# Four blocks of experts 0 to 3, with tokens of the first eleven tiles, ranked, gathered and begun ahead of the routing of the rest

## What is computed

```python
x = x + tanh(g_xattn) * xattn(layernorm(x), ctx, ctx, mask)      # 16 heads, 77 context rows
# _ffn on layernorm(x), B*S = 2048 tokens, E = 8 experts, D = 256, F = 1024
logits = xt @ Wr + br
gates  = max(softmax(logits)); idx = argmax(softmax(logits))     # top-1 routing
xn     = layernorm(xt) * ln_g + ln_b
h      = relu(xn @ W1[idx] + b1[idx])
y      = (h @ W2[idx] + b2[idx]) * gates
x = x + tanh(g_ffn) * y
```

## Time and profile before

| | |
|---|---|
| median of 3 runs | 311.1 us (309.79 to 313.14) |
| profiled execution | 310.44 us, of which the span of the core is 308.6 us |
| mean granted TensorE clock | 0.965 |
| PE busy | 280.3 us, 91% |
| DVE busy | 193.1 us, 63% |
| ACT busy | 163.2 us, 53% |
| POOL busy | 137.6 us, 45% |

### The profile page before, as it was taken

One profiled execution on the slowest core, in us unless ns is written; L12 is line 12 of the kernel. 1 busy time (PEld: TensorE's weight loads), 2 busy tenths in 40 slices (PEclk: granted clock), 3 DMA queues, 4 the chain that ended last, 5 costly groups with the idle time before them and its releaser, 6 DMA issues.

```text
span 308.6 us, 7697 instructions
## 1 busy us (share of the span) xinstructions
PE 280.3 (91%) x2489; PEld 249.3 (81%) x2489; DVE 193.1 (63%) x640; ACT 163.2 (53%) x439; POOL 137.6 (45%) x265
## 2 busy tenths in 40 slices
PE   7899998999999999999476999999999999999980
PEld 3668887888888888888234999888899989999970
DVE  3578589989999999886883653433435443445540
ACT  2243566767767777674316694434255725544440
POOL 2425247777777755434424653222232543322221
PEclk9999999999999999997777999999999999999996
DMA  6999994100103555551124303111121112112120
GB/s 139 295 296 372 377 379 135 54 37 35 37 36 129 174 202 173 179 170 43 37 75 135 101 11 88 54 30 48 52 56 55 50 54 57 54 59 80 55 58 14
DMA packets 19851, 34.59 MB, mean 112 GB/s; under 512 B 2518, under 2 KB 14612, under 8 KB 19801
## 3 DMA queue, kind: packets, MB, share of 16 engines
q1 hardware_dynamic: 15513, 21.28, 21.3%
q0 software_dynamic: 4144, 12.62, 13.0%
q10 hardware_dynamic: 144, 0.07, 0.1%
HBM read 27.60 MB, written 6.75 MB: 111 GB/s over the span
## 4 chain that ended last, share of the span: by engine, by line
PE 60%; DVE 24%; issue 6%; DMA 3%; ACT 2%; POOL 2%; SPq 1%; DVEq 1%; POOLq 0%; ACTq 0%
PE pS L1638 22%; PE pB L1709 15%; DVE mx L849 5%; PE pB L1445 4%; PE pA L1338 4%; PE pB L1426 4%; DVE Pb L857 3%; PE pT L1338 3%; DMA cst<-in_consts_dram 2%; DVE xs L879 2%; DVE st L884 1%; DMA zin<-rows_dram,idxg 1%; DVE xh L827 1%; PE pS L1382 1%; PE pA L1361 1%
## 5 line engine op out<-in xcount | busy, mean ns | idle before, releaser
L1638 PE MATMUL pS<-znf,W1c 128*128 128x128 f32 x576 | 72.2, 280 | 0.4 <-DVE W1c L1221 0.4
L1638 PEld LDWEIGHTS pS<-znf,W1c 128*128 128x128 f32 x576 | 68.7, 196 | 3.2 <-issue 3.2
L1709 PE MATMUL pB<-W2p,hT 128*128 128x256 f32 x408 | 53.7, 286 | 0.0
L1242 DVE TENSOR_SCALAR hA<-pS,b1s 128x128 f32<-128x128 f32 x72 | 20.3, 344 | 51.8 <-PE pS L1638 38.6
L1709 PEld LDWEIGHTS pB<-W2p,hT 128*128 128x128 f32 x408 | 50.0, 190 | 1.4 <-issue 1.2
L408 POOL DMA_INDIRECT out_dram<-yo,idxs x17 | 17.7, 1039 | 72.6 <-DVE yo L1270 63.9
L724 ACT ACTIVATE hA<-pS,b1s 128x128 f32<-128x128 f32 x72 | 20.6, 368 | 46.4 <-PE pS L1638 46.4
L1426 PE MATMUL pB<-VB,PT 128*128 128x51 f32 (+1 forms) x320 | 37.8, 273 | 0.4 <-DVE xs L879 0.3
L1426 PEld LDWEIGHTS pB<-VB,PT 128*128 128x128 f32 (+1 forms) x320 | 36.9, 192 | 1.4 <-issue 1.2
L567 ACT ACTIVATE Pb<-Pb 128x616 f32<-128x616 f32 x32 | 23.0, 718 | 17.3 <-DVE Pb L857 17.1
L391 POOL DMA_INDIRECT zin<-rows_dram,idxg x21 | 20.8, 992 | 16.5 <-issue 11.3
(11 more groups left out here) (233 smaller groups left out, 490.5 us busy)
## 6 DMA issues: line engine op xcount, KB each, us to landing
W1s<-in_L_ffn_W_dram SPq DMA_DIRECT2D x8, 1024.0 KB, 9.8
W2s<-in_L_ffn_W_dram SPq DMA_DIRECT2D x8, 1024.0 KB, 10.9
rows_dram<-pay POOLq DMA_DIRECT2D x16, 260.0 KB, 2.5
xs<-in_x_dram SPq DMA_DIRECT2D x3, 512.0 KB, 7.8
W2s<-in_sel_dram SPq DMA_DIRECT2D x1, 385.0 KB
zin<-rows_dram,idxg POOLq DMA_INDIRECT x21, 3.3
out_dram<-yo,idxs POOLq DMA_INDIRECT x17
W1s<-in_L_xattn_wk_dram SPq DMA_DIRECT2D x1, 256.0 KB, 3.1
```

Of the source, the lines that this page charges most:

```text
L1638: t = e.matmul(pS[:, 2 * (s % 2) + n, 128 * c:128 * c + 128], W1c[k][n][:, 128 * c:128 * c + 128], znf[s % 2][:, 128 * k:128 * k + 128], s ...
L1709: t = e.matmul(o, hT[s % 2][a][:, 128 * c:128 * c + 128], W2p[b_][c // 2][:, D * (c % 2):D * (c % 2) + D], start=False, stop=(c == 7 and a ...
```

## The change

Slots 0 to 3 become fixed: slot s is the first block of expert s (KA = 4), filled only with tokens of the first GA = 11 tiles, and only if these tiles hold at least 128 tokens of that expert. Otherwise its token numbers are all "none", and the slot is run all the same. The other slots are worked out as before over NL = 21 slots, with the counts less what the first blocks took; the total layout has NS = 25 slots, of which slots 4 and up start again at expert 0. The small path is hosted two slots behind the fixed ones (HOST = 6).

- The first group of ranks covers 11 tiles and moves into the loop (n = 13 on PE and DVE), with a product of counts for it; the key comparison for the four blocks (`first_values`) is in n = 14.
- `first_ids` on PE sits inside the `attend` of the last tile; then POOL gathers the four blocks between the steps of the last tiles' `rstd2` and `store_row`.
- The splits of W2 for slots 0 to 3 are done each time, pieces 1 to 3 on POOL and piece 0 on DVE; W1 is read without a copy.
- The work of slots 0 to 3 is written in between the steps of the routing of the rest, on all engines.
- SBUF buffers are reordered so that those of the first slots do not lie over attention's. Slots 0 to 4 share one pair of `hA` buffers.

```diff
-NS = 21
+KA = 4
+NL = 21
+NS = KA + NL
 FIRST = 14
-NK = NS + E
+NK = NL + E
+GA = NT - 5
-HOST = 2
+HOST = KA + 2
-WARM = (6, 3, 6, 9)
+WARM = (6, 3, 4)
...
-        groups = ((0, NT - 4), (NT - 4, NT - 1), (NT - 1, NT))
+        groups = ((0, GA), (GA, NT - 1), (NT - 1, NT))
...
 # POOL, after the loop
+            for x_ in range(KA):
+                e.wait_ge(d_W[x_], 32)
+            W2_low(0, 1)
+            e.wait_ge(g["dve_idxg"], 1)
+            for n in range(3):
+                i = GA - 1 - n
+                e.wait_ge(rsem[i % 3], 16 * (i // 3 + 1))
+            gather(0)
             rstd2(y)
+            gather(1)
+            gather(2)
+            rstd2(z)
             store_row(y - 1)
-            rstd2(z)
+            e.wait_ge(g["pe_PV"], NT)
+            gather(3)
             store_row(y)
             store_row(z)
+            W2_low(0, 2)
+            W2_low(0, 3)
+            for c in range(1, 4):
+                W2_low(1, c)
-            e.wait_ge(g["dve_idxg"], 1)
+            e.wait_ge(g["dve_idxg"], 2)
...
-            for s in range(4):
-                gather(s)
+            gather(KA)
+            gather(KA + 1)
+            e.wait_ge(g["dve_idxs"], 1)
+            scatter(0)
+            for c in range(1, 4):
+                W2_low(2, c)
+            scatter(1)
+            gather(KA + 2)
             e.wait_ge(g["dve_slot"], 1)
+            for c in range(1, 4):
+                W2_low(3, c)
+            scatter(2)
+            gather(KA + 3)
...
 # ACT, after the loop
+            copy_OT(y)
+            copy_PT(z, 0)
...
+            W2_high(0, 0)
+            W2_high(0, 1)
+            copy_PT(z, 1)
+            copy_PT(z, 2)
...
+            gate_exp(y)
+            W2_high(0, 2)
+            W2_high(0, 3)
+            x2_row(z)
+            e.wait_ge(g["dve_lnb"], 1)
+            layer_in(0)
+            z_row(z)
+            layer_in(1)
+            gate_exp(z)
+            e.wait_ge(g["dve_b1"], 1)
+            relu(0)
+            high(0, 0)
+            high(0, 1)
+            relu(1)
+            layer_in(2)
...
+            high(1, 0)
             for hf in range(2):
                 e.wait_ge(g["dve_ohs"], hf + 1)
                 i0, i1 = HALVES[hf]
                 e.activation(R[:, i0:i1, 0, :], ohs_half[hf], ACT.Copy, scale=cv("pcol")).then_inc(g["act_R0"], 1)
+            high(1, 1)
+            for c in range(4):
+                W2_high(1, c)
+            relu(2)
+            layer_in(3)
+            high(2, 0)
+            high(2, 1)
+            for c in range(4):
+                W2_high(2, c)
             e.wait_ge(g["dve_slot"], 1)
-            regs(0)
+            regs(KA)
...
+            relu(3)
+            high(3, 0)
+            high(3, 1)
+            for c in range(4):
+                W2_high(3, c)
+            layer_in(KA)
...
 # DVE: which of the first blocks are full
+            def first_blocks():
+                e.scalar_tensor_tensor(out=kdE, in0=cnt_first[:, 0:KA], scalar=127.5, in1=cv("k17")[:, 0:KA],
+                                       op0=ALU.is_lt, op1=ALU.add).then_inc(g["dve_own"], 1)
+                own.up()
+                e.tensor_scalar(taken[:, 0:KA], cnt_first[:, 0:KA], 127.5, 128.0, ALU.is_gt, ALU.mult).then_inc(
+                    g["dve_first"], 1)
...
 # DVE, in the loop and after it
+                if n == NT - 3:
+                    e.wait_ge(g["pe_xT"], NT - 1)
+                    early = rank(0)
+                    next(early)
+                    first_blocks()
+                if n == NT - 2:
+                    for _ in range(3):
+                        next(early)
+                    first_values()
...
             together(router(z), rank(1))
             gate(z)
+            e.wait_ge(g["dve_b1"], 1)
+            relu(0)
             more = rank(2)
             e.wait_ge(g["pe_rank"], 3)
...
             for _ in more:
                 pass
+            low(0, 0)
+            low(0, 1)
             e.wait_ge(g["dve_own"], t_s)
...
+            relu(1)
+            out_rows_of(0)
+            low(1, 0)
+            low(1, 1)
+            W2_low(1, 0)
-            e.wait_ge(g["pe_ids"], 1)
+            e.wait_ge(g["pe_ids"], 2)
...
 # PE, after the loop
+            e.wait_ge(g["dve_Sm"], 2 * NT)
+            warm(WARM[2], pS[:, 2, :])
+            transpose_O(y)
+            transpose_P(z, 0)
+            project(y)
+            transpose_P(z, 1)
+            transpose_P(z, 2)
+            attend(z, range(4))
+            first_ids()
+            attend(z, range(4, NC))
+            counts(0)
+            transpose_O(z)
+            project(z)
+            ranks(1)
+            counts(1)
+            transpose_z(0)
+            hidden(0, 0)
+            transpose_z(1)
+            hidden(0, 1)
+            counts(2)
+            ranks(2)
+            hidden(1, 0)
+            transpose_z(2)
+            hidden(1, 1)
+            output(0, (0, 1))
+            late_ids()
+            hidden(2, 0)
+            transpose_z(3)
+            hidden(2, 1)
+            output(1, (0, 1))
+            rest_ids()
+            hidden(3, 0)
+            hidden(3, 1)
+            output(2, (0, 1))
+            late_bias()
+            transpose_z(KA)
...
-            for s in range(FIRST):
+            for s in range(KA - 1, FIRST):
                 slot(s)
```

More of the change, by code:

```diff
@@ L1113, in _ @@
-            early = rank(0)
-            together(router(y - 1))
-            resid(y)
-            stats2(y)
-            for _, _ in zip(range(9), early):
-                pass
-            norm(z)
-            gate(y - 1)
-            logits(y)
-            together(router(y))
-            resid(z)
-            stats2(z)
-            for _ in early:
-                pass
-            gate(y)
-            logits(z)
-            together(router(z), rank(1))
-            gate(z)
-            more = rank(2)
@@ L1271, in out_rows_of @@
                                        in1=zi[:, 256:512], op0=ALU.mult, op1=ALU.add).then_inc(g["dve_y"], 1)
+            y, z = NT - 2, NT - 1
+            few = {}
+            together(router(y - 1))
+            e.wait_ge(g["pool_iota"], 1)
+            for _ in range(GA + 1):
+                next(early, None)
+            resid(y)
+            stats2(y)
+            e.wait_ge(g["pe_ids"], 1)
+            e.tensor_copy(idtE, idsE[:, 1, :]).then_inc(g["dve_own"], 1)
+            e.wait_ge(g["dve_own"], own.up())
@@ new lines, in _ @@
+            e.tensor_copy(b1s[:, :, 0:KA], pS[:, 2, 0:8 * KA].rearrange("p (c s) -> p c s", c=8)).then_inc(
+                g["dve_b1"], 1)
+            gate(y - 1)
+            logits(y)
+            together(router(y))
+            resid(z)
+            stats2(z)
+            gate(y)
+            for x_ in range(KA):
+                e.wait_ge(d_W[x_], 32)
+            W2_low(0, 0)
+            e.wait_ge(g["dve_first"], 2)
+            e.scalar_tensor_tensor(out=kadj, in0=taken[:, 1:9], scalar=float(KEY), in1=taken[:, 0:8], op0=ALU.add,
+                                   op1=ALU.subtract).then_inc(g["dve_own"], 1)
@@ new lines, in _ @@
+            own.up()
+            e.tensor_scalar(kko, kk[:, 0:NL], taken[:, 0:1], None, ALU.add).then_inc(g["dve_own"], 1)
+            own.up()
+            logits(z)
+            together(router(z), rank(1))
+            gate(z)
+            e.wait_ge(g["dve_b1"], 1)
+            relu(0)
+            more = rank(2)
+            e.wait_ge(g["pe_rank"], 3)
+            e.tensor_scalar(pc, cnt, 31.5, ROUND, ALU.add, ALU.add).then_inc(g["dve_own"], 1)
+            e.wait_ge(g["dve_own"], own.up())
@@ new lines, in _ @@
+            out_rows_of(1)
+            low(2, 0)
+            low(2, 1)
+            W2_low(2, 0)
+            e.wait_ge(g["pe_ids2"], 1)
+            e.tensor_copy(idt2, ids2[:, 1, :]).then_inc(g["dve_own"], 1)
+            t = own.up()
+            e.tensor_scalar(emp2, ids2[:, 2, :], 0.5, 8192.0, ALU.is_lt, ALU.mult).then_inc(g["dve_own"], 1)
+            t_e = own.up()
+            e.wait_ge(g["dve_own"], t)
+            e.tensor_tensor(idxg[:, NS:NS + 2], idt2, ids2[:, 0, :], ALU.add).then_inc(g["dve_idg2"], 1)
@@ L1418, in attend @@
                     e.wait_ge(g["dve_VB"], 2)
-                for c in range(NC):
+                for c in chunks:
                     n = chunk_rows(c)
@@ L1598, in _ @@
-            project(z)
-            ranks(1)
-            counts(1)
-            counts(2)
-            ranks(2)
-            e.wait_ge(g["dve_x2"], NT)
-            warm(WARM[2], pS[:, 2, :])
-            for hf in range(2):
-                e.wait_ge(g["dve_ohr"], NT)
-                e.wait_ge(g["act_PT"], 3 * NT)
-                e.wait_ge(g["act_R0"], hf + 1)
-                e.wait_ge(g["dve_R1"], hf + 1)
-                for i in range(*HALVES[hf]):
-                    t = e.matmul(ids, ohr[:, i, :], R[:, i, :, 0:NS], start=(i == 0), stop=(i == NT - 1))
```

556 lines of the change are left out of this document (307 added, 249 removed).

## The result

The changed kernel takes **335.07 us** (median of 5 runs, 332.14 to 335.91) against 310.43 us for the kernel before beside it (309.79 to 313.14): a ratio of **1.077 [1.073, 1.082]**, some 24.6 us slower. The forecast was 322.0 us, with a range to 328. The direction and its reason stood; the size was off by 13 us. The profiled execution is the slowest of the five, 335.91 us with a span of 333.8, so it is laid against the span of 308.6: +25.2 us, where my sum gave +11.0.

A forecast was written before the change was run, and what follows sets the result against it. PE was taken to bound attention and expert stage, with room only in the middle; +20.3 - 14.4 + 1.9 + 1.4 + 1.8 = +11.0 us on 310.44 gave 321.4, put at 322.0 us, range 316.5 to 328.

The forecast's parts named there:

- Part 1: Expert stage: three of four fixed slots are empty and still run, 20 slots at 6.77 us each, +20.3 us.
- Part 4: Early slots: PE waits added by the change's order, +1.4 us at `late_ids` and +1.8 us before `hidden(4, 0)`.
- a doubled clock cost: First W1 products: slow-clock start costing some 1.7 us could vanish or come twice, kept for the range.
- my bounds of 0 and 7: Early slots: limits in us for the two added waits together.
- Part 2: Head start: first W1 product at 152.7 instead of 167.1 us, -14.4 us, bounds -15.8 and -11.6.
- Part 3: Routing work moved among the slots now uses PE's time, +1.9 us, bounds 1.5 and 2.5.
- Part 5: W2 splits in each early slot, three pieces on POOL: costed at nothing, covered by 3.6 us of hidden products.
- The rule of the shared port: Early slots: two-input DVE and SBUF-reading POOL instructions take turns, adding DVE's three subtractions to POOL's line; up to rival B's time.
- rival B: POOL's line of splits bounds slots 1 to 4, 8.6 against 6.77 us each, +7, so 329 us; chance 0.14.
- the copy of 964 ns: Trace before: DVE's W1 copy, median 428 ns, took 964 over POOL's W2 piece; cited as sign of port sharing.

The follow-up runs named there:

- plus3: The kernel before with three empty slots appended at its end, nothing early; 331.73 us, ratio 1.064.
- real: The changed kernel with its four fixed slots given to two full blocks each of experts 2 and 4, 17 slots run; 315.04 us, ratio 1.005.
- dvelow: The changed kernel with all low W2 pieces of slots 0 to 3 made by DVE, none by POOL; 335.99 us, ratio 1.074.
- layer: The changed kernel with `layer_in(4)` on ACT moved ahead of the last half of slot 3's relu and its four W2 copies; 331.7 us, scattered.
- warm: The changed kernel with filler products on PE, four ahead of `hidden(0, 0)` and sixteen in the wait ahead of `hidden(4, 0)`; 330.4 us, ratio 1.069.
- later: The changed kernel with POOL's first W2 piece moved from ahead of the first gather to behind the last row store; 334.33 us, ratio 1.071.
- reallayer: real with layer's order: four full fixed blocks and `layer_in(4)` moved up; 309.11 us, ratio 0.999.
- once: reallayer with one W2 split for the two blocks of an expert; 306.31 us, ratio 0.989.
- best: once with four filler products before `hidden(0, 0)` and four in the wait before `hidden(4, 0)`; 304.66 us, ratio 0.983.
- best_ids: best with `low(0, .)` ahead of DVE's last ranking and `late_ids` on PE behind `hidden(2, 0)`; 303.69 us, ratio 0.975.
- after_again: The changed kernel run once more, unedited; 337.85 us, ratio 1.085.
- best_dve: best with the early low W2 pieces, eight in all, made by DVE instead of two by DVE and six by POOL; 302.85 us, ratio 0.973.
- best_both: best with the edits of both best_dve and best_ids; 300.8 us, ratio 0.970.
- stack: The changed kernel, empty slots kept, with the edits of later and layer and the fillers of best; 329.67 us, ratio 1.066.

## Why the prediction missed, by its own steps

**Part 1, slots, +20.3: right.** plus3 gives +20.2 for three empty slots alone, real takes 20 to 21 us off. The count of 20 slots held.

**Part 4, added waits, +3.2: the term that failed most.** Its first wait, forecast +1.4 at `late_ids`, came as 0.92 in `output(0)` and 0.72 at `late_ids`, together 1.6: right in size, partly by luck, as the first wait is another one, for DVE's `low(0, 0)` behind the operation of 1.55 us, and the sum did not have it. The second, `layer_in(4)`, was forecast at +1.8 and measured 4.62. I counted the last two W2 copies and the scaling, on the footing that ACT would be waiting there with the rest done. What I did not follow is the path one engine further back: DVE's `relu(3)` is written behind the copy of `b1s`, that waits for `late_bias` on PE, and that stands behind `output(2)`. So `relu(3)`, though its products were long done, ran only after `output(2)` had ended at 187.4, and then came in series 1.1 us of relu on DVE, 0.6 on ACT, 2.2 for four copies and 0.8 of scaling, to 192.7.

dvelow shows the link (DVE idle for 6.63 us before that copy), layer shows the order (0.90 with `layer_in` moved up). And the wait took the clock down: 6.7 us for two halves instead of 4.0, +2.7, as warm shows (+1.8 to 2.0 in the other executions with this wait). I had kept a doubled clock cost for the range alone. The waits by themselves, 6.3 us, lie inside my bounds of 0 and 7; with the clock they are 1.6 + 4.6 + 2.7 = 8.9 where the sum had 3.2.

**Part 2, head start, -14.4: overstated by 3.9.** The comparisons "fit in the 1.81 us that DVE waits": alone they take 1.88, but POOL's piece, which the change issues at that moment, stretched them to 2.94 and PE waited 2.14 us. later takes the piece away and both shrink. From the last tile's scores to the first W1 product it was 22.99 and 22.42 us in two executions of the change, and 20.2 to 21.2 in the twelve variants, in none of which a piece lay over the comparisons, against 20.2 by my sum: about 2.2 us of the miss. They are the wait, 1.1 us longer than in later, and the lower clock behind it, 2.78 us for the last twelve products of `attend` instead of 1.52; `resid(z)`, which I had near 150.5, came at 154.8. The sum had neither.

In the variants that leave this piece in its place (layer, warm, real, reallayer, once, best, best_ids) it fell just behind the comparisons, as ACT's copies for it came 0.8 to 1.3 us later against them; a start that depends on such an offset is fragile. Another 1.1 us were there before any of the change's work at the end (tile 3's scores stood at 43.14 us, at 42.03 before) and differ between executions of one program. The last 0.6 I cannot assign.

**Part 3, routing among the slots, +1.9: not contradicted.** `late_ids` took 0.78 and `rest_ids` 0.87 in the change. In five other executions `rest_ids` had three to five gaps, and in three of them (after_again, real, dvelow) the products behind ran at a lower clock; together that was 3.5 to 5.7 us, for which the sum had no term. The change's profiled execution has none of it.

**Part 5, re-splits, 0: short by 0.4 in the change.** That is PE's wait for the pieces of slots 0 to 3. once gives 1.4 us for each re-split taken out, but in reallayer's order, where PE waited 1.9 us for pieces as in layer: the cover held only as long as something else was later.

**The rule of the shared port.** In the change DVE operations of 0.15 us on tiles of 128 x 8, x 20, x 21 and x 2 took 1.55, 1.23, 1.32 and 4.35 us, each under POOL's pieces, and none is over 0.5 us in dvelow, best_dve and best_both, where the early pieces are DVE's. So POOL's line delayed DVE, not the reverse: the 18 pieces have a mean of 1.32 us, 1.29 before. I had let this stand for rival B, with POOL's line as the bound, and that did not come: PE waited 0.43 us for a piece in slots 0 to 3, not 7. The Trainium skill, "SBUF — State Buffer", section "Who interferes with whom", calls the pair of ports that VectorE and GpSimd share an exclusive lock; these rows agree with it in kind. They go beyond the form in my prediction: one operation stood through three pieces, and the comparisons and the operations of 1.55 and 1.32 us have one input, as has the copy of 964 ns that I gave as its sign. I had applied the rule to big subtractions, and it decided at the smallest operations of the routing chain, on the path.

**The rest, 2.3 us**, had no term: 0.8 around slot 5 (of it 0.4 for the small path's transposes, which the kernel before had in the middle piece, and 0.16 of waiting for a POOL piece), 1.25 behind the last `output` (13.62 us against 12.37), the remainder unassigned. Nor is 1.7 us of the middle piece assigned: 20.3 + 1.9 + 6.7 of waits + 2.9 of clock behind the big one (6.8 us to `output(3)` against 3.9 in layer) are 31.8 of 33.5. Some 0.6 of it is the slow start, 7.6 us for the first 48 W1 products where the kernel before took 7.0. What is left stays open. The mistake was one of kind in the working: I priced each wait by the last thing ahead of it, where several engines' written orders form one chain.

## What to carry to other kernels

Count what an unconditional early step runs on before what it gains: here three of four early blocks were empty, and at 6.8 us each that was more than the head start, forecast at 14.4 us and measured at 10.5. With four full blocks and the orders mended the same idea gained 9.6 us. When work is moved into another engine's order, follow the wait back through every engine until you reach one that is really busy; behind the longest wait here stood the written order of a small copy (`b1s`). Price a wait of PE with the clock behind it (here 4.6 us of wait brought 1.8 to 2.7 more), and look for the small operations that share a port with the moved work.

## What the hardware showed that I had not expected

A DVE operation of 0.15 us on 128 x 2 elements took 4.35 us in the change (2.64 to 3.76 in six other executions), longer than one POOL piece of 1.3: it stood through three of them in a row. A one-input `tensor_scalar` on 128 x 8 floats was held up too (3.66 us in stack). Four filler products ahead of the first block were enough for it to run at the full clock (1.95 us for sixteen products in best, 3.54 in once, the same kernel without fillers). The gaps inside `rest_ids`, most of 0.52 to 0.56 us, came in some executions (after_again, layer, real, dvelow, best_ids) and not in others (the change's first, later, stack, warm, reallayer, once, best, best_dve, best_both); behind them the granted clock fell to 0.68 in after_again and 0.59 in dvelow, while in layer and best_ids the next products kept their 3.84 us. No run here tells why.
